# Heads turned by the DMA engines, one row maximum over four banks, and casts and opening weight work moved between engines, in a gated cross-attention and ternary feed-forward kernel

## The reference

```python
x = x + tanh(g_xattn[0]) * xattn(ctx, layernorm(x), fside, fside, ...)
x = x + tanh(g_ffn[0]) * ffn(layernorm(x), ...)

def xattn(x, latents, shift, scale, ...):      # x: (32, 375, 256), latents: (32, 112, 256)
    xn, ln = layernorm(x)*w1+b1, layernorm(latents)*w2+b2
    q, kv = ln @ Wq, xn @ Wkv                  # 16 heads of 64
    k, v = split(kv)
    q = q * (1 + scale) + shift                # per batch and head
    attn = softmax(q k^T / 8)
    return (attn v) @ Wout

def bitlinear(x, w, b):                        # 256 -> 1024 -> 256
    xq = act_quant(rmsnorm(x))                 # 8 bit levels, one scale per row
    wq = weight_quant(w)                       # ternary, one scale per matrix
    return xq @ wq^T + b

def ffn(x): return bitlinear(gelu(bitlinear(x, w1, b1)), w2, b2)
```

## Time and profile before

| | us |
|---|---|
| median of three runs | 1119.94 |
| the profiled execution | 1121.15 |
| its span, first to last instruction | 1119.3 |
| TensorE busy | 1068.0 (95%) |
| ScalarE busy | 970.7 (87%) |
| VectorE busy | 946.4 (85%) |
| GpSimd busy | 772.1 (69%) |
| mean granted TensorE clock, as a share of full | 0.986 |

### The profile page before, as it was taken

The page is one execution under the profiler, slowest core; times in us unless marked ns, Lnnn a source line. Parts: engine busy times, 40 slices in busy tenths (PEclk is TensorE's granted clock), DMA queues, the critical chain, the costliest instruction groups (busy, mean ns, idle before and its releaser), DMA issues.

```text
span 1119.3 us, 32134 instructions
## 1 busy us (share of the span) xinstructions
PE 1068.0 (95%) x11910; PEld 733.5 (66%) x11910; DVE 946.4 (85%) x2112; ACT 970.7 (87%) x1865; POOL 772.1 (69%) x837
## 2 busy tenths in 40 slices
PE   3999999999999999999999999999999999999994
PEld 2566767666766766776766676776666676666662
DVE  5897788988888888888898878898888888888884
ACT  5788799999999799999999979999999988999762
POOL 3566676777667678767677766777766767777552
PEclk9899999999999999999999999999999999999996
DMA  8456667757667865687775575775667686654550
GB/s 272 86 109 107 101 106 122 123 97 126 115 114 118 133 104 101 123 115 110 134 119 99 120 118 99 122 127 104 115 119 120 109 137 112 97 124 106 112 114 24
DMA packets 408153, 129.08 MB, mean 115 GB/s; under 512 B 389792, under 2 KB 402848, under 8 KB 408000
## 3 DMA queue, kind: packets, MB, share of 16 engines
q1 hardware_dynamic: 408000, 127.03, 64.1%
HBM read 26.71 MB, written 3.67 MB: 27 GB/s over the span
## 4 chain that ended last, share of the span: by engine, by line
PE 78%; ACT 9%; DMA 5%; issue 3%; DVE 2%; POOL 1%; POOLq 0%; DVEq 0%; SPq 0%; ACTq 0%
PE work L844 16%; PE work L846 16%; PE work L845 16%; PE ps_s L863 11%; DMA pt<-pn 4%; PE ps_o L844 3%; PE ps_o L846 3%; PE ps_o L845 3%; PE work L927 3%; ACT prob L608 2%; ACT q_f L574 2%; ACT L608 2%; PE work L956 2%; PE work L918 2%; PE work L965 2%
## 5 line engine op out<-in xcount | busy, mean ns | idle before, releaser
L448 POOL TENSOR_TENSOR pn<-prob,pn 112x750 f16<-112x750 f32 x256 | 400.2, 1569 | 117.5 <-ACT pn L618 97.8
L608 ACT ACTIVATE prob<-ps_s,neg_max 112x375 f32<-112x375 f32 x512 | 265.1, 573 | 10.5 <-DVE neg_max L759 7.5
L759 DVE TENSOR_REDUCE neg_max<-ps_s 112x2 f32<-112x750 f32 x256 | 237.6, 929 | 21.6 <-PE ps_s L863 21.5
L844 PE MATMUL ps_o<-v_h,pt 128*128 128x65 f16 (+1 forms) x1536 | 166.5, 194 | 9.1 <-DMA pt<-pn 7.6
L844 PE MATMUL work<-z,wkv_h 128*128 128x375 f16 x512 | 168.4, 329 | 2.7 <-POOL z L469 2.5
L681 DVE SCALAR_TENSOR_TENSOR k_l<-work,k_h 128x375 f16<-128x375 f32 x256 | 136.4, 541 | 38.4 <-ACT k_h L530 38.3
L530 ACT ACTIVATE k_h<-work 128x375 f16<-128x375 f32 x256 | 121.4, 488 | 53.4 <-PE work L846 48.6
L846 PE MATMUL work<-z,wkv_l 128*128 128x375 f16 x512 | 167.2, 327 | 0.0
L845 PE MATMUL work<-z,wkv_h 128*128 128x375 f16 x512 | 166.8, 326 | 0.0
L845 PE MATMUL ps_o<-v_l,pt 128*128 128x65 f16 (+1 forms) x1536 | 166.3, 192 | 0.0
L846 PE MATMUL ps_o<-v_h,pt 128*128 128x65 f16 (+1 forms) x1536 | 166.3, 193 | 0.0
(11 more groups left out here) (135 smaller groups left out, 2723.5 us busy)
## 6 DMA issues: line engine op xcount, KB each, us to landing
ctx_in<-in_ctx SPq DMA_DIRECT2D x32, 375.0 KB
pt<-pn SPq DMA_TRANSPOSE x256, 3.5
x_in<-in_x SPq DMA_DIRECT2D x32, 112.0 KB, 3.8
x_res<-in_x SPq DMA_DIRECT2D x28, 128.0 KB, 5.0
out<-y SPq DMA_DIRECT2D x28, 128.0 KB, 2.0
stage<-in_wkv SPq DMA_DIRECT2D x2, 1024.0 KB, 9.3
stage<-in_w SPq DMA_DIRECT2D x2, 1024.0 KB, 13.1
stage<-in_wq SPq DMA_DIRECT2D x1, 1024.0 KB, 8.2
```

What stands on the lines that cost most here:

```text
L448: g.tensor_tensor(buf[:, 1, :, 0:SK], prob[:, p % 2], buf[:, 0, :, 0:SK], ALU.subtract).then_inc(p_lo, 1)
L608: i = a.activation(prob[:, p % 2, h, :], ps_s[0:SQ, 2 * (p % 2) + h, 0:SK], ACT.Exp, bias=neg_max[:, 2 * (p % 2) + h:2 * (p % 2) + h + 1])
L759: v.tensor_reduce(neg_max[:, 2 * (p % 2):2 * (p % 2) + 2], ps_s[0:SQ, 2 * (p % 2):2 * (p % 2) + 2, 0:SK], X, ALU.max, negate=True).then_in ...
L844: t_.matmul(dst, sh, mh, start=(n == 0), stop=False)
```

## The change

- OO0, OO1 leave TensorE's lists and the work banks. OH now waits for `o_normed` and casts half of `attn` (512 columns) from SBUF into a new tile `an`, on ScalarE. OL is new, on GpSimd: it subtracts for the low part of `an`. OT is now a DMA transpose of `an` (112x1024, both parts) straight into `ot`, issued by SyncE between the transposes of the pairs. WO waits for both transposes of the last batch that it reads (`o_turned`). N waits for the OL of the batch before, OH for the OT of the batch before.
- `CAST_ACT` is (0, 2, 4): pair 6 is cast on VectorE.
- M0, M2, M4, M6 stay, and each takes the maxima of two pairs, over all four banks of `ps_s`; M1, M3, M5, M7 go. Both exponentials wait for the one reduce, and the reduce for both scores.
- At the opening, WOL and TN0, TN1 are done on GpSimd, the first as two instructions (scale, subtract).
- All lists are rewritten. Of the lists only the new ORDER is shown here; FIRST and LAST hold the same steps for the first and the last batches.

```diff
-CAST_ACT = (0, 2, 4, 6)
+CAST_ACT = (0, 2, 4)
...
 ORDER["PE"] = [
+    ("K5", 0), ("A2", -1), ("A3", -1), ("Z1", 1), ("K4", 0), ("K6", 0), ("A4", -1), ("S0", 0),
+    ("S1", 0), ("K7", 0), ("V01", 0), ("V00", 0), ("A5", -1), ("Q1", 0), ("ZX", 1), ("S2", 0),
+    ("S3", 0), ("K0", 1), ("A6", -1), ("V02", 0), ("K1", 1), ("A7", -1), ("K2", 1), ("F0", -2),
+    ("V11", 0), ("V10", 0), ("K3", 1), ("F1", -2), ("A0", 0), ("A1", 0), ("S4", 0), ("S5", 0),
+    ("F2", -3), ("V12", 0), ("WO", -1), ("Z0", 2), ("Q0", 1), ("S6", 0), ("S7", 0),
 ]
...
 ORDER["ACT"] = [
+    ("OH0", -1), ("XR", -2), ("KH7", 0), ("VH01", 0), ("E0", 0), ("VH00", 0), ("E1", 0), ("QF1", 0),
+    ("PH0", 0), ("KH0", 1), ("ZXF", 1), ("VH02", 0), ("E2", 0), ("KH1", 1), ("PH2", 0), ("KH2", 1),
+    ("E3", 0), ("OH1", -1), ("VH11", 0), ("LNW", 2), ("VH10", 0), ("KH3", 1), ("GE", -2), ("VH12", 0),
+    ("E4", 0), ("PH4", 0), ("E5", 0), ("SQ", -2), ("ZF0", 2), ("QF0", 1), ("KH5", 1), ("E6", 0),
+    ("E7", 0), ("ZF1", 2), ("KH6", 1), ("KH4", 1), ("HR", -2),
 ]
...
 ORDER["DVE"] = [
+    ("M2", 0), ("KL0", 1), ("XTE", -2), ("BS", 2), ("VL02", 0), ("KL1", 1), ("N3", -1), ("KL2", 1),
+    ("HE0", -2), ("HTE", -3), ("VL11", 0), ("PH3", 0), ("HE1", -2), ("VL10", 0), ("N0", 0), ("KL3", 1),
+    ("M4", 0), ("YE", -3), ("HMX", -2), ("VL12", 0), ("X1", -1), ("XST", -1), ("PH5", 0), ("M6", 0),
+    ("N1", 0), ("KL5", 1), ("SC2", -2), ("PH6", 0), ("PH7", 0), ("KL6", 1), ("KL4", 1), ("SC1", -1),
+    ("M0", 1), ("KL7", 1), ("VL01", 1), ("BA", 3), ("VL00", 1), ("N2", 0), ("BB", 3), ("PH1", 1),
 ]
...
 ORDER["POOL"] = [
+    ("PL0", 0), ("PL1", 0), ("QS1", 0), ("LNA", 2), ("OL1", -1), ("PL2", 0), ("PL3", 0), ("ZXS", 1),
+    ("PL4", 0), ("RM2", -2), ("RM1", -1), ("PL5", 0), ("QS0", 1), ("ZS0", 2), ("PL6", 0), ("XB", -1),
+    ("XQ", -1), ("PL7", 0), ("ZS1", 2), ("OL0", 0), ("HQ", -2),
 ]
...
 ORDER["SP"] = [
+    ("ST", -5), ("T0", -1), ("T1", -1), ("OT0", -2), ("OT1", -2), ("T2", -1), ("T3", -1), ("T4", -1),
+    ("LD", 2), ("T5", -1), ("LX", 2), ("T6", -1), ("RS", -1), ("XD", -2), ("T7", -1), ("HD", -3),
 ]
...
         attn = sb("attn", [SQ, INNER])
+        an = [sb(f"an{i}", [SQ, 2, HALF], F16) for i in range(2)]
...
         o_normed, o_hi, q_ready = sem("o_normed"), sem("o_hi"), sem("q_ready")
+        o_lo = sem("o_lo")
+        o_turned = [sem(f"o_turned{i}") for i in range(2)]
...
+            def turn_heads(b, half):
+                sp.wait_ge(o_lo, 2 * b + half + 1)
+                if b == 0:
+                    sp.wait_ge(lo_split[3], 1)
+                for t in last_user(b):
+                    sp.wait_ge(full[BANK["WO", t]], USE["WO", t])
+                sp.dma_start_transpose(ot[:, half].rearrange("p a c q -> p (a c) q")[:, :, columns(b)],
+                                       an[half][:].rearrange("p a n -> p (a n)")).then_inc(o_turned[half], 16)
+
...
                     turn(b, int(name[1]))
+                if name[0:2] == "OT":
+                    turn_heads(b, int(name[2]))
...
+            def split_heads(b, half):
+                pool.wait_ge(o_hi, 2 * b + half + 1)
+                g.tensor_tensor(an[half][:, 1], attn[:, half * HALF:(half + 1) * HALF], an[half][:, 0], ALU.subtract).then_inc(o_lo, 1)
+
...
+            def split_output_weights():
+                pool.wait_ge(hi_split[3], 1)
+                g.tensor_scalar(wout_f, wout_f, W_SCALE, 0.0, ALU.mult, ALU.add)
+                pool.drain()
+                g.tensor_tensor(wout_l[:], wout_f, wout_h[:], ALU.subtract).then_inc(lo_split[3], 1)
+
+            def ternary(n):
+                w = (w1_f, w2_f)[n]
+                pool.wait_ge(tern_rounded[n], 1)
+                g.tensor_scalar(w, w, -ROUND, 1.0, ALU.add, ALU.min)
+                pool.drain()
+                g.tensor_scalar((w1_t, w2_t)[n][:], w, -1.0, 1.0, ALU.max, ALU.min).then_inc(tern_ready[n], 1)
+
             def step(name, b):
+                if name == "WOL":
+                    split_output_weights()
+                if name in ("TN0", "TN1"):
+                    ternary(int(name[2]))
...
                     split_p(b, int(name[2]))
+                if name[0:2] == "OL":
+                    split_heads(b, int(name[2]))
...
                 if name[0:2] == "OH":
-                    job, half = ("OO" + name[2], b), int(name[2])
-                    act.wait_ge(full[BANK[job]], USE[job])
-                    if b == 0:
-                        act.wait_ge(lo_split[3], 1)
-                    for t in last_user(b):
-                        act.wait_ge(full[BANK["WO", t]], USE["WO", t])
-                    a.activation(ot[:, half, 0, :, columns(b)],
-                                 work[:, BANK[job], 0:4 * SQ].rearrange("p (c q) -> p c q", c=4), ACT.Identity).then_inc(o_hi, 1)
+                    half = int(name[2])
+                    act.wait_ge(o_normed, 4 * b + 2 + 2 * half)
+                    if b > 0:
+                        act.wait_ge(o_turned[half], 16 * b)
+                    a.activation(an[half][:, 0], attn[:, half * HALF:(half + 1) * HALF], ACT.Identity).then_inc(o_hi, 1)
...
                     g = b * PAIRS + p
-                    act.wait_ge(max_ready, g + 1)
+                    act.wait_ge(max_ready, g // 2 + 1)
...
-            def ternary(n):
-                w = (w1_f, w2_f)[n]
-                dve.wait_ge(tern_rounded[n], 1)
-                v.tensor_scalar(w, w, ROUND, 1.0, ALU.subtract, ALU.min)
-                dve.drain()
-                v.tensor_scalar((w1_t, w2_t)[n][:], w, -1.0, None, ALU.max).then_inc(tern_ready[n], 1)
-
...
                 dve.drain()
+                if b > 0:
+                    dve.wait_ge(o_lo, 2 * b + quarter // 2 - 1)
...
                     split_lo(2, wkv_f[:, :, INNER:2 * INNER], wkv_h[:, :, INNER:2 * INNER], wkv_l[:, :, INNER:2 * INNER])
-                if name == "WOL":
-                    split_lo(3, wout_f.rearrange("p (a k) n -> p a (k n)", a=2), wout_h[:].rearrange("p (a k) n -> p a (k n)", a=2),
-                             wout_l[:].rearrange("p (a k) n -> p a (k n)", a=2))
...
                     weight_means()
-                if name in ("TN0", "TN1"):
-                    ternary(int(name[2]))
...
                     g = b * PAIRS + p
-                    dve.wait_ge(scored, g + 1)
-                    v.tensor_reduce(neg_max[:, 2 * (p % 2):2 * (p % 2) + 2], ps_s[0:SQ, 2 * (p % 2):2 * (p % 2) + 2, 0:SK], X, ALU.max, negate=True).then_inc(max_ready, 1)
+                    dve.wait_ge(scored, g + 2)
+                    v.tensor_reduce(neg_max[:], ps_s[0:SQ, :, 0:SK], X, ALU.max, negate=True).then_inc(max_ready, 1)
...
                     normalise_heads(b, int(name[1]))
-                if name[0:2] == "OT":
-                    job, half = ("OO" + name[2], b), int(name[2])
-                    dve.wait_ge(o_hi, 2 * b + half + 1)
-                    v.tensor_tensor(ot[:, half, 1, :, columns(b)], work[:, BANK[job], 0:4 * SQ].rearrange("p (c q) -> p c q", c=4),
-                                    ot[:, half, 0, :, columns(b)], ALU.subtract).then_inc(evacuated[BANK[job]], 1)
...
                         i = t_.transpose(w[:, c * SQ:(c + 1) * SQ], x_n[:, c * P:(c + 1) * P], ident[0:SQ, 0:SQ])
-                if name in ("OO0", "OO1"):
-                    pe.wait_ge(o_normed, 4 * b + 2 + 2 * int(name[2]))
-                    for m in range(4):
-                        c = 4 * int(name[2]) + m
-                        i = t_.transpose(w[:, m * SQ:(m + 1) * SQ], attn[:, c * P:(c + 1) * P], ident[0:SQ, 0:SQ])
...
                         pe.wait_ge(lo_split[3], 1)
-                    for half in ("OO0", "OO1"):
-                        results(last_batch(b), [half])
+                    for half in range(2):
+                        pe.wait_ge(o_turned[half], 16 * (last_batch(b) + 1))
```

9 lines of the change are left out of this document (3 added, 6 removed), and 190 rows, old and new, of the table CAST_ACT.

## The result

The kernel after took 1157.11 us (median; 1154.52 to 1158.35), the kernel before 1120.71 beside it: ratio 1.0326 (95% interval 1.0311 to 1.034). The forecast was 1098.5 with a range from 1087 to 1116. Both the sign and the range were wrong.

The account below looks back on a forecast made before the run. TensorE was taken as the bound from about 30 to 1080 us; the profiled span 1119.3 - 27.3 + 2.8 + 0 + 3 = 1097.8 us, + 1.85 - 1.2 = 1098.5 us, range 1087 to 1116.

Parts of the forecast that it names:

- TensorE -27.3 us: TensorE, batches before the tail: 62 removed head-turning jobs of 0.44 us each shorten the run by 27.3 us.
- the loop of scores: Scores wait for banks that exponentials read, behind one longer reduce; claimed 1.5 and 0.9 us to spare in its stretches.
- GpSimd's 82%: GpSimd per batch afterwards: 26.6 us of a 32.5 us period, so not the bound by its sum.
- VectorE 27.8 us per batch: VectorE's summed work per batch afterwards, 86% of a 32.5 us period, so not the bound.
- The third rival: Middle: VectorE and GpSimd block each other; VectorE at 31.7 us, stalls of 0.5 us per batch, 1111 us; chance 0.06.
- New waits +3 us, 0.1 per batch: Middle: new waits from the longer reduce and fuller GpSimd add 3 us, bounds -3 and +15.
- First rival: Middle: the loop of scores becomes the path, costing 1.5 us per batch, 1141 us; chance 0.09.
- Second rival: Middle: DMA-turned heads land late and WO waits half a microsecond per batch, 1111 us; chance 0.12.
- Opening 0, bounds -3 and +5: Opening: weight work moved to GpSimd, some 5 us a step, is covered by idle time and costs 0.
- Tail +2.8, bounds 0 and +6: Last tokens: normalise to WO takes 5.3 us by the new way against 2.5, adding 2.8 us.
- Durations: Single instructions: reduces 1.70 us, casts of attn 0.60, subtractions of attn 1.16, new transposes landing after 3.2 to 3.5.

Follow-up runs that it names:

- b_oo1: Kernel before with one transpose instead of four in each of TensorE's jobs OO0 and OO1, nothing added: 1111.75 us, ratio 0.9924.
- a_pl1: Kernel after with opening weight work back on VectorE and GpSimd's eight long subtractions per batch cut to one column: 1111.86 us, ratio 0.9922.
- b_pl1: Kernel before with GpSimd's eight long subtractions per batch cut to one column: 1117.59 us, ratio 0.9978.
- a_max2: Kernel after with each four-bank maximum cut in two over two banks, each exponential waiting for its own: 1159.1 us, ratio 1.0343.
- a_both: Kernel after, opening weight work on VectorE, x minus mean for one column, pair 5's exponential ahead of pair 4's cast on ScalarE: 1143.38 us, ratio 1.0205.
- b_heads: Kernel before with only the heads turned by DMA, OL behind QS1 and PL2, OT behind T1 and T2: 1262.58 us, ratio 1.1264.
- a_mult: Kernel after with GpSimd's four ternary passes written with multiply and add instead of minimum and maximum: 1134.12 us, ratio 1.0141.
- b_heads2: Kernel before with only the heads turned by DMA, OH0, OL0 and OT0 earlier and OT1 ahead of the context load: 1141.2 us, ratio 1.0169.

## Why the prediction was wrong, step by step

**TensorE -27.3 us: the size of the job was right, its worth wrong.** "What it no longer does shortens the run until another chain is late" was the sentence it hung on; and the next chain was judged from sums of durations ("None becomes the bound by its sum") and from the loop of scores with 0.9 us to spare. b_oo1 shows that the kernel before gives back 40% of removed work, and in its middle 1.9 us of 16.5: 99% busy is no proof that all of a removed job comes back. Close behind TensorE stand GpSimd and the transfers, and the prediction took GpSimd's 82% for room.

**VectorE 27.8 us per batch: mis-sized by 2.2.** From the stretches, 624.04 of 700 us at 33.70 per batch are 30.0. In a_pl1 590.78 at 32.71 are 27.6, and ScalarE's 627.56 are 29.3 (forecast 29.8). So the sums of durations were right for a VectorE without the eight subtractions beside it, and with that VectorE the full period is 32.67, inside the forecast 32.5 to 32.7.

**The third rival was the one, at 0.06.** Its mechanism stands; it spoke of VectorE at 31.7 and 0.5 us of stalls per batch. Measured: 30.0, and 33.73 less 32.67 is 1.06 us per batch. Its chance was read from the casts alone, "most don't wait now". That was true of the order before, and it was the new order that was to be judged. I had left out that short instructions pay most: x minus mean and the variance step grew to about four times their length (345 to 1308 ns, 221 to 895), and both were in the trace at or near their undisturbed length. The sign was there all the same, in rows that I didn't read: two scale factors of one element took 1.01 and 0.66 us in the kernel before, and take 0.22 and 0.29 in b_pl1.

**New waits +3 us, 0.1 per batch: the step that failed in the middle.** It is the same omission: blocking costs 1.06 us per full period.

**First rival** (scores, 0.09): a_max2 says no. Its distances were incomplete all the same: between S5 and S6 ScalarE also does VH12 and a table load of 1.28 us. A loop made of that was my second theory. a_both gave it no support, but doesn't refute it either, since the casts grew by 11.8 us in the same stretch.

**Second rival** (heads late): not in the kernel after, where WO waits 0.2 us in all for the transposes of the heads, which land 2.9 us after their issue. It came true in b_heads, by my placing.

**Opening 0, bounds -3 and +5: measured +15.3.** The step that failed is "GpSimd does each pass in some 2 to 4 us, at 1 to 2 ns per element (the pairs take 2)". No instruction of before has a minimum or maximum on GpSimd, and the nearest rows, of another kind of operation, were no bound for them. At 1.9 us a pass (a_mult) the opening is 5.5 us shorter than before.

**Tail +2.8, bounds 0 and +6: measured +5.7.** Timelines of the last tokens, as the earlier trace rows:

```profile
1117.78 0.42 DVE L714 TENSOR_TENSOR attn<-ps_o,row_inv 112x256 f32<-112x256 f32 x1
...
1118.24 0.63 ACT L594 ACTIVATE an<-attn 112x512 f16<-112x512 f32 x1 [0.96 <-DVE attn L714]
...
1125.19 0.42 PE L858 MATMUL work<-wout_h,stage 128*128 128x256 f16 x1
...
1130.21 0.48 DVE L807 SCALAR_TENSOR_TENSOR x<-work,tanh_xs,x_res 128x256 f32<-128x256 f32 x1 [3.37 <-PE work L860]
```

From the end of the normalise (1118.20) to WO it is 7.0 us in place of the forecast 5.3, as a feed-forward job started in front of WO on TensorE at 1123.53, four matmuls of 512 columns at 0.42 us each, the lower level; WO itself then takes 5.0 in place of 2.9, 2.1 more, where the upper bound allowed 2.6 for the lower clock.

**Durations:** maximum 1.71 (forecast 1.70), cast of attn 0.66 (0.60), subtraction 1.16 (1.16), landing of the new transposes 2.9 (3.2 to 3.5). Those were right or near and didn't decide.

**What stays open.** The middle came out 34.5 us above the forecast (842.42 for 807.9): 17.9 go with the eight subtractions, 6.9 with the opening weight work, and 9.8 have no shown cause. a_pl1's middle has 32.71 us per batch where 32.2 (33.10 less 0.88) would have been the full gain. And the time that b_heads2 doesn't win was not traced to one cause. Its casts and its variance step are longer than in the kernel before (0.68 for 0.59 us, 0.42 for 0.22), its two scale factors together are not (1.70 for 1.67), and its waits for the pairs' transposes have tripled; none of it was tested there.

## What to carry to other kernels

Where two engines exclude each other, a reordering is a change of cost, and neither engine's sum of durations shows it: compare each short instruction's mean with its shortest, and count every place where it may now meet a long one of the other engine. Price an operation that moves to another engine by a row of the same kind of operation on that engine, not by its element count alone. Before a removed job is booked as a gain, ask how far the next engine is behind; here one at 99% busy gave back 40% at most. And a subtraction held back to spare another engine is late for its own readers: look at both.

## What the runs showed of the hardware

- GpSimd: a one-input pass over 128x2048 f32 takes 1.90 us with multiply and add, 7.1 with a minimum or maximum in it, at the same shape and place.
- VectorE instructions of one to three elements per partition wait up to 1.1 us for GpSimd's work: 0.92 for 125x3 in place of 0.17, 1.29 for 128x1 in place of 0.16.
- The two-input form waits with both tiles in SBUF (1.45 us for 256 elements; the shortest took 0.48) and not with one in PSUM (0.53 to 0.55 for 375, also beside GpSimd's subtractions).
